# Other steps and buffers for the feed-forward weight pieces in a three-part decoder layer on one core

## The reference

```python
x = _layernorm(x + autocorrelation(x))            # corr by FFT, top 6 lags, weighted shifted sum
# cross attention: 32 heads of 128, 2 batches seen as rows of 8 blocks
x = _rmsnorm(hidden_states, ln_weight)
h_q = (x @ w_q.T); h_k = (key_value_states @ w_k.T); h_v = (key_value_states @ w_v.T)
score = einsum('bqhd,bkhd->bhqk', h_q, h_k) + position_bias
score = softmax(where(mask, score, -inf))
x = _layernorm(x + hidden_states + einsum('bhqk,bkhd->bqhd', score, h_v) @ w_out.T)
# feed-forward
logits = hidden_states @ gate_w; routing_weights = top_k(logits, 2)
shared_out = relu(hidden_states @ up_w) ** 2 @ down_w
expert_out = (hidden_states @ fc1_w) @ expert_w * sum(routing_weights)
x = _layernorm(x + _layernorm(shared_out + expert_out @ fc2_w, ln_gamma, ln_beta))
```

## Time and profile before

| | |
|---|---|
| median of three runs | 1025.45 us (1023.52 to 1027.25) |
| the profiled execution | 1023.36 us, span 1021.6 us |
| PE busy | 989.8 us, 97% of the span |
| DVE, POOL, ACT busy | 721.8, 555.7, 518.6 us |
| mean granted TensorE clock | 0.993 |
| DMA | 119.81 MB, mean 117 GB/s |

### The profile page before, as it was taken

How to read it: one execution, slowest core, us unless ns; L and a number is a source line. 1 busy time by engine, 2 the same in 40 slices (tenths; PEclk the granted TensorE clock), 3 DMA queues, 4 the chain that set the end, 5 groups by cost and what they waited for, 6 DMA issues and landing times.

```text
span 1021.6 us, 18521 instructions
## 1 busy us (share of the span) xinstructions
PE 989.8 (97%) x5652; PEld 860.7 (84%) x5652; DVE 721.8 (71%) x1710; ACT 518.6 (51%) x1276; POOL 555.7 (54%) x504
## 2 busy tenths in 40 slices
PE   9999999999999988999999999999999999989996
PEld 8888788799999986888888888888888887768785
DVE  6768676665566657878787878787787878762526
ACT  7745444532232236656666666666566666344160
POOL 0345776554445348766576556666665766343113
PEclk9999999999999999999999999999999999999999
DMA  7543445364534345223333233342234323100011
GB/s 268 179 152 124 155 166 174 125 227 145 181 140 155 135 150 195 89 90 105 126 105 107 88 108 105 105 128 87 91 104 126 105 69 131 64 1 1 1 42 41
DMA packets 57585, 119.81 MB, mean 117 GB/s; under 512 B 7232, under 2 KB 11328, under 8 KB 57536
## 3 DMA queue, kind: packets, MB, share of 16 engines
q1 hardware_dynamic: 57536, 119.19, 34.5%
HBM read 83.51 MB, written 35.65 MB: 117 GB/s over the span
## 4 chain that ended last, share of the span: by engine, by line
PE 70%; DVE 3%; POOL 3%; ACT 1%; DMA 1%; issue 1%; SPq 0%; POOLq 0%; DVEq 0%; ACTq 0%
PE psum L1833 20%; PE psum L1835 19%; PE psum L1834 19%; PE psum L1839 7%; PE psum L1840 3%; PE psum L1999 2%; DMA raw<-in_ffn 1%; POOL wvq_lo L880 1%; DMA v_blocks<-rows 0%; POOL stat L912 0%; POOL smx L760 0%; DVE rsum L1732 0%; ACT smx L1172 0%; DVE st L1742 0%; DVE smx L1740 0%
## 5 line engine op out<-in xcount | busy, mean ns | idle before, releaser
L707 POOL TENSOR_TENSOR mix<-kf,mix 128x512 fp32r<-128x512 f32 x64 | 83.9, 1311 | 165.5 <-ACT mix L958 165.5
L1833 PE MATMUL psum<-mix,av_hi 128*128 128x256 f32 (+1 forms) x496 | 172.3, 347 | 0.0
L1833 PE MATMUL psum<-xn_lo,ext_hi 128*128 128x512 f32 x256 | 104.5, 408 | 1.0 <-POOL ext_lo L707 1.0
L1833 PEld LDWEIGHTS psum<-mix,av_hi 128*128 128x128 f32 x496 | 94.8, 191 | 7.7
L1835 PE MATMUL psum<-xn_hi,ext_hi 128*128 128x512 f32 x256 | 100.7, 393 | 0.0
L1834 PE MATMUL psum<-xn_hi,ext_lo 128*128 128x512 f32 x256 | 100.3, 392 | 0.0
L1172 ACT ACTIVATE smx<-smx,nmin 128x128 f32<-128x128 f32 x256 | 99.2, 393 | 1.9 <-DVE nmin L1476 1.9
L1835 PE MATMUL psum<-mix,av_hi 128*128 128x512 f32 x240 | 95.0, 396 | 0.0
L1834 PE MATMUL psum<-mix,av_lo 128*128 128x512 f32 x240 | 94.5, 394 | 0.0
L958 ACT ACTIVATE mix<-psum 128x512 fp32r<-128x512 f32 x70 | 41.8, 599 | 92.9 <-PE psum L1835 90.1
L1503 DVE TENSOR_TENSOR acc<-psum,acc 128x512 f32<-128x512 f32 x128 | 87.1, 682 | 0.1
(11 more groups left out here) (269 smaller groups left out, 3183.2 us busy)
## 6 DMA issues: line engine op xcount, KB each, us to landing
kf<-k_blocks SPq DMA_DIRECT2D x64, 256.0 KB, 2.7
wvq_hi<-v_blocks SPq DMA_DIRECT2D x64, 256.0 KB, 2.9
raw<-in_wk SPq DMA_DIRECT2D x16, 512.0 KB, 3.6
k_blocks<-far SPq DMA_DIRECT2D x32, 256.0 KB, 2.2
raw<-in_wv SPq DMA_DIRECT2D x16, 512.0 KB, 4.2
v_blocks<-rows SPq DMA_DIRECT2D x32, 256.0 KB, 2.2
raw<-in_wq SPq DMA_DIRECT2D x16, 512.0 KB, 3.3
raw<-in_wo SPq DMA_DIRECT2D x16, 512.0 KB, 3.3
```

Source lines behind the costliest of these rows:

```text
L707: g.tensor_tensor(dst_lo, src, dst_hi, ALU.subtract).then_inc(s_lo, 1)
L1833: mm(out, lhs(0), rhs(1), start=first, stop=False)
```

## The change

1. In the first pair of heads ACT takes the high parts of `UP[0]` and `UP[1]` at the end of steps 2 and 3, not of steps 0 and 1; POOL takes both low parts in step 3, not one in step 1 and one in step 3.
2. Before the first step ACT does the exponentials of unit 0 ahead of the high parts of the values of units 0 and 1.
3. In the last pair POOL waits, before it starts on the output weights and `UP[2]`, `UP[3]`, for the probabilities of unit 62, and before `FC1` and what follows for those of unit 63. The output weights now come first.
4. The `DOWN` pieces lie elsewhere: the first in `kf`, the next two in `av`, the last in `wvq`. ACT splits the first in step 3 of the last pair, the next two between the high parts of the turned tiles, the last after `up_act(0, 1)`. POOL takes the low parts of the first three, in one run once four tiles are normed, and then adds beta to four tiles before it turns to the inverse roots of tiles 4 to 7; DVE takes only the last.

```diff
-        BY_VECTOR = (8, 10)
+        BY_VECTOR = (10,)
...
-                    if is_first(g) and j in (1, 3):
-                        split_low(UP[j // 2])
+                    if is_first(g) and j == 3:
+                        split_low(UP[0])
+                        split_low(UP[1])
                     if last and j == 1:
+                        pool.wait_ge(s_probs_ready, units - 1)
+                        wo_lo(g)
                         split_low(UP[2])
-                        wo_lo(g)
                         split_low(UP[3])
+                        pool.wait_ge(s_probs_ready, units)
                         split_low(FC1)
...
-            ffn_lo(DOWN[0])
+            pool.wait_ge(s_x2_ready, HB)
+            for k in DOWN[0:3]:
+                ffn_lo(k)
+            for tile in range(HB):
+                add_beta(tile)
             for tile in range(HB, B):
                 y_power(tile)
-            ffn_lo(DOWN[2])
-            for tile in range(B):
+            for tile in range(HB, B):
                 add_beta(tile)
...
+            exps_of(0, 0)
             v_hi(0, 0, 0)
             v_hi(1, 0, 1)
-            exps_of(0, 0)
...
                     hi_of(s_t_mm, s_t_hi, n + 1, flat(pt[0]), psT[:, :])
+                    if last and j == 3:
+                        ffn_hi(DOWN[0])
...
-                    if (is_first(g) or last) and j < 2:
-                        ffn_hi(UP[j + (2 if last else 0)])
+                    if is_first(g) and j >= 2:
+                        ffn_hi(UP[j - 2])
+                    if last and j < 2:
+                        ffn_hi(UP[j + 2])
...
-            for tile in range(HB):
-                x2_hi(tile)
+            x2_hi(0)
+            x2_hi(1)
+            ffn_hi(DOWN[1])
+            x2_hi(2)
+            x2_hi(3)
+            ffn_hi(DOWN[2])
             fused_hi()
...
-                if hf == 0:
-                    ffn_hi(DOWN[0])
                 up_act(hf, 1)
                 if hf == 0:
-                    ffn_hi(DOWN[1])
+                    ffn_hi(DOWN[3])
                 logits_copy(hf)
                 for c in range(2, IC):
                     up_act(hf, c)
-                    if hf == 0 and c in (2, 3):
-                        ffn_hi(DOWN[c])
...
                 up_lo(hf, 1)
                 if hf == 0:
-                    ffn_lo(DOWN[1])
                     for tile in range(HB, B):
                         x2(tile)
```

More of the change, by code:

```diff
@@ L450, in down_rows @@
             if c < 2:
[L451 to L454, removed]
+                return kf[:, i * PIECE + c * D:i * PIECE + (c + 1) * D]
+            if c < 6:
+                return av[i][:, 2 * PIECE + (c - 2) * D:2 * PIECE + (c - 1) * D]
+            return wvq[i][:, PIECE + (c - 6) * D:PIECE + (c - 5) * D]
         def ffn_dst(i, k):
@@ L466, in ffn_dst @@
             if k == DOWN[0]:
+                return kf[:, i * PIECE:(i + 1) * PIECE]
+            if k == DOWN[3]:
                 return wvq[i][:, PIECE:2 * PIECE]
-            if k == DOWN[1]:
-                return kf[:, i * PIECE:(i + 1) * PIECE]
-            n = 2 * PIECE + (k - DOWN[2]) * PIECE
+            n = 2 * PIECE + (k - DOWN[1]) * PIECE
             return av[i][:, n:n + PIECE]
@@ L1224, in ffn_hi @@
                 if k == DOWN[0]:
+                    act.wait_ge(s_k_lo, units)
+                if k in DOWN[1:3]:
+                    act.wait_ge(s_a_mm, units)
+                if k == DOWN[3]:
                     act.wait_ge(s_fused_mm, LC)
[L1226 to L1229, removed]
                 copy_hi(ffn_dst(0, k), ffn_src(k)).then_inc(s_f_hi, 1)
```

## The result

The changed kernel took 1017.64 us (median of 6 runs, 1016.03 to 1018.34), the kernel before beside it 1024.51 (6 runs, 1022.67 to 1028.16). The ratio is 0.9926, 95% interval 0.9912 to 0.9940. That is 7.6 us less by the ratio, and 6.9 as the difference of the two medians. The forecast was a gain of 4.6, to 1020.9; from the lower median of before in this comparison, 1020.9 is only 3.6 away. The profiled execution took 1017.27 us, and the span of the profiled executions fell from 1021.6 to 1015.4, by 6.2.

A forecast was written before the change was run, and what follows sets the result against it. PE, busy for 97% of the span, was taken to bound the kernel. Terms 1.4 - 1.2 + 1.4 + 3.0 = 4.6 us took the median 1025.45 to 1020.9; forecast's own range 1019 to 1022.5, overall 1017 to 1024.5.

The forecast's parts named there:

- the price of the clock at the second norm: Output product at 879 runs at half speed after PE's wait: a loss of 0.9 to 2.2 us, middle 1.55.
- first steps: First attention steps: unit 1 attended 0.4 us sooner and the query weights' waits of 1.0 gone, 1.4 gained.
- last pair: Last pair through second norm: 0.35 us gained at the first tile, 1.55 lost to the clock, a loss of 1.2.
- wait for `DOWN[0]`: Feed-forward part: PE's wait of 1.36 us at 902 goes, 1.4 gained.
- logits' sums: Feed-forward part: DVE's four logit sums no longer run against POOL's work, 3.0 us gained, bounds 2.0 and 3.0.
- The 1.0 for the query weights: First steps: POOL no longer carries UP[0] in step 1, so 1.0 us of waits for query weights goes.
- the 3.8 saved at the turning: Last pair: 2.1 us from turning without a wait and 1.7 from no lower clock after 864, none expected to last.
- The first rival: Steps 2 and 3: the two UP pieces hold unit 4's sums and normalisation; gain 2.9, time 1022.6; 25%.
- the hold didn't pay in full: Rival, last pair: the hold saves 3.8 us and there is no clock fall at 879; time 1015.9; 7%.
- the clock didn't hold at the norm: Rival, second norm: the clock holds at 879; gain 4.6 + 1.55, time 1019.3; 10%.
- nor stay low: Rival, after 879: clock stays low through fuse and first chunks, 23 us, losing 4.5; time 1030; 6%.
- the sums were freed: Opposing rival, feed-forward: logit sums stay held by POOL's adds; gain 1.6 at the least, time 1023.8; 6%.

The follow-up runs named there:

- e7: The changed kernel plus 16 transposes on PE, with results nobody reads, in its wait before the second norm: 1016.29 us, ratio 0.9918.
- e11: The changed kernel without edit 2, so the value high parts of units 0 and 1 again precede unit 0's exponentials: 1016.47 us, ratio 0.9905.
- e8: The changed kernel with POOL taking the bias of unit 1 ahead of the low part of value block 0: 1014.93 us, ratio 0.9904.
- e10: The changed kernel plus 22 unread transposes on PE in step 0, between turning and attending unit 0: 1015.51 us, ratio 0.9902.
- e3: The kernel before with edit 3 alone, POOL held in the last pair and output weights first: 1026.92 us, ratio 1.0016.
- e5: The changed kernel without edit 3, POOL's holds and order in the last pair as before: 1016.97 us, ratio 0.9923.
- e4: The kernel before with edit 4 alone, the DOWN pieces in new buffers and new places in the queues: 1019.28 us, ratio 0.9945.
- e2: The kernel before with edit 2 alone, exponentials of unit 0 ahead of the first value blocks: 1024.84 us, ratio 0.9996.
- e1: The kernel before with edit 1 alone, UP[0] and UP[1] moved to steps 2 and 3: 1022.97 us, ratio 0.9981.
- e6: The changed kernel with the inverse roots of tiles 0 and 1 ahead of FC2 on POOL: 1017.19 us, ratio 0.9928.
- e9: The changed kernel with inverse roots of tiles 0 and 1 ahead of FC2 on POOL, and FC2 held until tile 1 is normed: 1013.70 us, ratio 0.9889.
- e12: The changed kernel with e8, e9 and 10 of the transposes of e7 together: 1011.81 us, ratio 0.9869.

## Why the prediction was right or wrong

The direction was right and so was nearly every mechanism; the size was not: 4.6 forecast, 6.2 between the two profiled executions, 7.6 by the ratio (6.9 by the medians). Two steps of the prediction failed. In its sum, the price of the clock at the second norm was put at 1.55 where the trace shows 0.85, and a removed wait at its idle time where the traces show 0.16 to 0.33 more each; these two make the 1.5 us from 4.6 to the traces' 6.1. And the gain of one trace was carried to the median as it was, which missed up to another 1.4. By terms, each as the move of one instruction from trace to trace:

| term | forecast | measured |
|---|---|---|
| first steps (turnings of the middle units) | 1.4 | 1.90 |
| last pair (fused copies, less the above) | -1.2 | -0.60 |
| wait for `DOWN[0]` (copy of the gate's logits, less the above) | 1.4 | 1.69 |
| logits' sums (ACT's first work on `up` chunk 4, less the above) | 3.0 | 3.13 |

- **First steps.** Unit 0 late by 0.7 (0.84 measured), low clock, unit 1 gaining 0.4 (0.45): right. The prediction had the normalisation of unit 0 at 377.7 to 379.0, held by POOL, which does not go with its own 4 us of waiting between turning and attending; it ran at 375.99 for 0.69, not held, and the late bias alone made the scores late. The 1.0 for the query weights was mis-sized: the two waits of 0.27 and 0.75 were worth 0.48 and 0.97. The row shows PE's idle time, but behind such a wait the first products run thinner too: after the wait of 1.36 at 901.94 the first two followed each other at 0.81 us instead of 0.68. With the 2.97 (3.13 measured), each removed wait gave 0.16 to 0.33 more than its idle. That the thinner start makes all of it is likely and not shown.
- **Last pair.** The chain was right at every link: sums held by `UP[3]`, FC1 after the probabilities, 0.26 gained at the first tile (0.35 forecast), 2.98 of waiting (3.7 forecast), the fall. The failing term is the clock's price, 1.55, the middle between 0.9 and 2.2. It was 0.85, the lower end: the fall began at 874.3, still in the wait, and 2.8 of its 6.8 us had passed over idle time and turnings when the output product began; of the rest the 0.81 of waiting that stood there before hid a part. e7 measures it. But 0.85 is one draw: from the output product to the fused copies, against the 10.42 of before, the fall behind a wait of 2.97 to 2.99 cost 1.14 in e11, 1.02 in e8, nothing in e10, and 1.70 in e3, where a stretch of the same 6.8 us began at 880.5, only 1.0 before the output product. Of these five prices four lie below the forecast's middle, and two below its lower bound of 0.9. e5 shows that the 3.8 saved at the turning really do not last.
- **Feed-forward.** Right, and the largest part, as e4 shows.
- **Steps 2 and 3.** The normalisation of unit 4 was held 2.62 us (405.58 above), the sums weren't, and PE's slack took it. The first rival needed both.
- **From the profiled execution to the median.** The forecast carried 4.6 from one to the other unchanged. Two things differ between executions at places that the change touches. One is the landing of `UP[0]`. In the kernel before ACT waits for it, and four traces that share this code have its high part start at 385.26 (e4), 386.01 (before), 386.36 (e2) and 387.12 (e3), and unit 1 attended at 390.12, 390.86, 391.21 and 391.97: what the landing is late comes straight through. Edit 1 takes it off the path. The other is the clock, which the sum took to hold at 917 in every execution. Behind the wait of 2.97 at 917 it held in the traces of before and e2, and fell for 3.4 us in those of e1 and e3. From the end of this wait to ACT's first work on `up` chunk 6 it took 13.03 and 13.04 us in the first two, 14.66 and 14.62 in the others. So 1.6 us more go with edit 4 in those executions, and the trace read for the forecast was one without this fall. Of 29 executions of the kernel before that were timed beside e1 to e4, 12 had a mean granted clock of 0.992 or 0.993 and a median of 1023.79 us, the other 17 had 0.987 to 0.990 and 1026.18.

Which of the two made the difference is not shown. The runs of edit 1 alone gained 1.9, which is no more than the two traces show for edits 1 and 2 together, and still spread over 4.4 us; those of edit 4 alone gained 5.6, where the traces show 4.8. This speaks for the clock, but each of these gains is uncertain by more than the 0.8 between them. That the changed kernel's six runs lie within 2.3 us, against 5.5, goes with either.

The sum of the four edits taken alone is 1.9 + 0.4 - 1.6 + 5.6 = 6.3 by their ratios, each uncertain by 1 to 1.7 us; the whole is 7.6, so they may add up and need not. That edit 3 costs less in company is in line with e5 but not shown. The other rivals fell: the hold didn't pay in full, the clock didn't hold at the norm nor stay low, and the sums were freed. The prediction set the row at 917 against the rule of the Trainium skill (TensorE: Matmul & The Clock Gate, "Why this matters for your kernels") that an idle gap in the matmul stream brings the clock down. At the norm the trace agrees with it, behind a wait of 2.98 us. At 917, behind 2.97, two traces of four agree and two do not, so the row showed one case and no exception. The Trainium skill's rule that of VectorE and GpSimd the one that starts first holds the other for its whole length (SBUF — State Buffer, "Who interferes with whom") agrees with e6 and e9, where the norms took 3.13 and 1.15.

## What to carry to other kernels

Before an instruction is moved ahead on one engine, look at what stands behind its old and its new neighbours in the next engine's queue: edit 2 gained nothing because a bias stood behind a value block on POOL, and e8 took the bias from there by moving one line. A wait in front of a bound engine that a queue's order causes is better cured by the order (e9) than by holding other work back (edit 3), and a held piece is to start right after, not right as, the other engine's short work. Where a DMA's landing, or a wait behind which the clock may fall, is on the path, one profiled execution gives one sample of it. Look at the same place in several traces, and at the granted clock of every run, before you carry a gain from a trace to the median.

## What was not expected of the hardware

- The same wait of 4.05 us in the same code had a low stretch of 6.8 us in the changed kernel, e5, e6 and e7, and one of 3.4 in e9, beginning at 379.4, 381.1, 379.2, 381.3 and 381.4 (from windows of half a us). Unit 1 was attended at 390.41, 391.16, 390.19, 391.19 and 389.54. With the bias first it was 387.94 with a stretch of 3.4 (e8) and 386.27 without one (e12): 1.67 us, half of 3.4. So the same code gave ends up to 1.65 us apart.
- The same holds of other waits. Behind the wait of about 2.1 before unit 62 is turned the clock fell for 3.4 us in the traces of before, e1, e4 and e5, and not in e2's, where it fell at the second norm instead (879.4), behind waits of 1.20, 0.35 and 0.71. Behind the 2.97 at 917 it fell in two traces of four.
- A `TENSOR_SCALAR` of DVE with one tensor input (the norm, 128 x 512; the sums, 128 x 4) is held by a POOL `TENSOR_TENSOR` of 128 x 1024 just as DVE's two-input `TENSOR_TENSOR` is: 3.13 for two norms instead of 1.15, and 2.27 for the sums instead of 0.16. The prediction had used this for the sums; the expectation of e6 had not looked for it at the second norm.
